# Window attention in a four-layer kernel: four heads side by side on groups of 32 array rows, scores formed twice, no transposes

## The reference

```python
win = pad(layer_norm(x)) cut into 14x14 windows        # 16x16 padded to 28x28: 4 windows an image, 196 places each
q, k, v = split(win @ qkv_w + qkv_b)                   # 12 heads of 16 channels
attn = einsum('nqc,nkc->nqk', q, k) * 0.25
attn = attn + (q . rel_pos_h)[..., :, None] + (q . rel_pos_w)[..., None, :]
o = einsum('nqk,nkc->nqc', softmax(attn), v)
x = x + o @ proj_w + proj_b
x = x + gelu(layer_norm(x) @ fc1_w + fc1_b) @ fc2_w + fc2_b
```

## Time and profile before

| what | us |
|---|---|
| median of 3 runs | 423.51 (423.33 to 425.48) |
| the profiled execution, its own time | 425.65 |
| its span | 423.9 |
| first attention: relative terms done to first matmul of fc1 | 42.9 to 144.0 |
| second attention: the same | 234.7 to 335.7 |

### The profile page before, as it was taken

One profiled execution on the slowest core, in us unless ns is written; L12 is line 12 of the kernel. 1 busy time (PEld: TensorE's weight loads), 2 busy tenths in 40 slices (PEclk: granted clock), 3 DMA queues, 4 the chain that ended last, 5 costly groups with the idle time before them and its releaser, 6 DMA issues.

```text
span 423.9 us, 7574 instructions
## 1 busy us (share of the span) xinstructions
PE 395.2 (93%) x2686; PEld 310.0 (73%) x2686; DVE 216.7 (51%) x631; ACT 206.2 (49%) x708; POOL 151.1 (36%) x197
## 2 busy tenths in 40 slices
PE   5499669999999999999999759999999999999997
PEld 2149668888888646977958758888888646986656
DVE  6843238777776810134763228776776800141272
ACT  1042238998888443013042328898888453021220
POOL 9441027776665630000042018776666300000000
PEclk9999959999999999999999959999999999999999
DMA  6616999200000102010005970000000000000002
GB/s 161 93 13 126 140 169 252 50 2 2 2 2 0 39 0 55 3 57 0 2 0 109 148 123 2 2 2 2 2 1 2 2 0 0 2 0 2 0 1 76
DMA packets 8424, 17.42 MB, mean 41 GB/s; under 512 B 1909, under 2 KB 5430, under 8 KB 8386
## 3 DMA queue, kind: packets, MB, share of 16 engines
q1 hardware_dynamic: 8386, 16.93, 20.6%
HBM read 9.68 MB, written 0.79 MB: 25 GB/s over the span
## 4 chain that ended last, share of the span: by engine, by line
PE 86%; DMA 7%; DVE 5%; issue 0%; ACT 0%; SPq 0%
PE bank L658 16%; PE bank L734 9%; PE bank L687 8%; PE bank L743 7%; DMA qaug<-arena 6%; PE bank L613 6%; PE bank L712 5%; PE bank L626 5%; PE bank L665 4%; PE bank L664 3%; DVE norm_or_q L1101 3%; PE bank L586 2%; PE bank L903 2%; PE bank L832 2%; PE bank L842 2%; PE bank L756 2%
## 5 line engine op out<-in xcount | busy, mean ns | idle before, releaser
L545 POOL TENSOR_TENSOR probs<-probs,recip 98x392 f32<-98x392 f32 x96 | 80.6, 840 | 34.6 <-DVE recip L1163 33.9
L968 ACT ACTIVATE probs<-bank,negmax 98x196 f32<-98x196 f32 x192 | 80.5, 432 | 9.8 <-DVE negmax L1152 9.4
L658 PE MATMUL bank<-kaug,qaug 100*98 100x196 f32 x384 | 81.1, 334 | 0.0
L1152 DVE TENSOR_REDUCE negmax<-bank 98x2 f32<-98x392 f32 x96 | 53.7, 559 | 23.1 <-PE bank L658 23.1
L658 PEld LDWEIGHTS bank<-kaug,qaug 100*98 100x98 f32 x384 | 55.6, 164 | 7.3 <-ACT probs L968 5.0
L547 POOL TENSOR_SCALAR probs<-probs,recip 112x112 f32<-112x112 f32 (+1 forms) x48 | 28.0, 583 | 62.2 <-DVE recip L1163 60.7
L687 PE MATMUL bank<-ident,probs 98*98 98x98 f32 x384 | 47.5, 247 | 0.2
L687 PEld LDWEIGHTS bank<-ident,probs 98*98 98x98 f32 x384 | 40.2, 127 | 4.2 <-issue 0.5
L734 PE MATMUL bank<-yT,fc 96*128 96x512 f32 x96 | 41.9, 593 | 0.0
L968 ACT ACTIVATION_READ_ACCUMULATOR probs<-bank,negmax 98x1 f32 x192 | 40.9, 213 | 0.0
L973 ACT ACTIVATE probs<-bank,negmax 112x280 f32<-112x280 f32 (+1 forms) x48 | 24.5, 511 | 25.0 <-DVE negmax L1156 23.6
(11 more groups left out here) (151 smaller groups left out, 604.0 us busy)
## 6 DMA issues: line engine op xcount, KB each, us to landing
fc<-in_fc SPq DMA_DIRECT2D x4, 576.0 KB, 9.3
kaug<-arena SPq DMA_DIRECT2D x6, 346.0 KB, 4.4
qaug<-arena SPq DMA_DIRECT2D x4, 448.0 KB
qaug<-norm_or_q SPq DMA_DIRECT2D x24, 64.0 KB, 2.4
qaug<-arena SPq DMA_DIRECT2D x4, 224.0 KB
qkv<-in_qkv SPq DMA_DIRECT2D x2, 432.0 KB, 8.2
x_tok<-in_x SPq DMA_DIRECT2D x4, 192.0 KB, 3.6
inverse<-in_inverse SPq DMA_DIRECT2D x1, 768.0 KB
```

The lines of the kernel that those rows point to most:

```text
L545: pool.tensor_tensor(p, p, by.unsqueeze(2).broadcast_to([n, 2, cols // 2]), ALU.mult).then_inc(s.normed, 1)
L658: last = mm(bank[0:HALF_WIN, 2 * HALF_WIN * part:2 * HALF_WIN * (part + 1)], q[:, at:at + HALF_WIN], keys, start=True, stop=True)
L968: ins = run(m.probs[0:HALF_WIN, slot, cols], bank[0:HALF_WIN, cols], ACT.Exp, bias=m.negmax[0:HALF_WIN, slot, part:part + 1], accum_out=m. ...
L1152: ins = dve.tensor_reduce(m.negmax[0:HALF_WIN, slot], bank[0:HALF_WIN, 0:4 * HALF_WIN].rearrange("k (a n) -> k a n", a=2), AX, ALU.max, ne ...
```

## The change

The attention is rewritten. Four heads form a slot (three slots), and each head has a group of 32 array rows: 16 rows of q or k with 16 zero rows, so that two slots can share one k tile. The relative terms have a tile of their own, `m.r`, with 28 rows for a head, one row for the negated maximum and one for a mask. A group of the new loop is four heads on one window set: 12 main and 6 edge groups a layer (`GROUPS`).

For a group, `score` forms queries by keys in banks 0 to 3, one head a bank: for a main group two blocks of 128 queries (all 256 places of the image), each as a product with k and one with the 0/1 table of keys, four heads side by side on the four row groups. `take_max` takes all maxima in one instruction and turns them with four 32x32 transposes on `dve`; `sp` moves them into row 28 of `m.r` (two small DMAs for a main group). `turn` then forms the scores again with keys first in banks 4 to 7, with the maximum already subtracted by that row, `act` takes exp of each bank, and `weigh` multiplies with v, whose 16 columns of ones give the sums. `take_weighed` copies the sums beside the outputs, inverts them for all 128 rows and 196 queries, and multiplies. There are no transposes on `pe`, no multiplication on `pool`, no copies of transposed blocks and no assembly DMAs; `pool` prepares the tiles of the edge groups instead. `out_project` has three products per tile instead of two, and `load_late` is issued as soon as the qkv weights have landed.

```diff
-UNITS = [(IMAGES + s, 4 * q + n) for q in range(QUADS) for s in range(2) for n in range(4)]
-UNITS += [(b, h) for b in range(IMAGES) for h in range(HEADS)]
-N_UNITS = len(UNITS)
...
+RIGHT_WIN, LOW_WIN = IMAGES, IMAGES + 1
+GROUPS = [(slot, b) for slot in range(2) for b in range(IMAGES)]
+GROUPS += [(slot, b) for slot in range(SLOTS) for b in (RIGHT_WIN, LOW_WIN)]
+GROUPS += [(SLOTS - 1, b) for b in range(IMAGES)]
+N_GROUPS = len(GROUPS)
+AHEAD = 3
+P_RING = 2
+M_RING = 3
...
-                            sp.dma_start(m.kaug[0:BIAS_ROW, quad, :], m.qkT[rows, chunk]).then_inc(s.aug[quad], 16)
...
-                        sp.dma_start(m.qaug[lo:lo + HD, head, :], m.qW[HD * n:HD * (n + 1), chunk]).then_inc(s.aug[head // 4], 16)
...
-                        sp.dma_start(m.qaug[lo:lo + WIN, heads, :], src[REL_ROWS[kind][g], g]).then_inc(s.aug_bias[g], 16)
...
+                wait_for(sp, s.proj_in, *taken_out(job("c", 2, 1)))
+                for j in range(4):
+                    sp.dma_start(m.k[GROUP * j:GROUP * j + HD, 1], m.k[GROUP * j + HD:GROUP * (j + 1), 1]).then_inc(s.k_moved, 16)
+                sp.wait_ge(s.edge_inputs, R_EDGES)
+                for n, (slot, b) in enumerate(GROUPS):
+                    sp.wait_ge(s.maxT, 4 * (n + 1))
+                    for part in range(max_moves(b)):
+                        n_max = 96 if part == 1 else 128
+                        if b < IMAGES:
+                            at = PLACES * b + 128 * part
+                            dst = m.r[MAX_ROW::GROUP, slot, at:at + n_max]
+                        else:
+                            dst = m.edgeR[MAX_ROW::GROUP, slot, b - IMAGES, :]
+                        sp.dma_start(dst, m.negmaxT[4 * part:4 * part + 4, n % M_RING, 0:n_max]).then_inc(s.max_rows[n % M_RING], 16)
             out_dram = out.rearrange("b h w c -> b (h w) c").rearrange("b (t p) c -> b p t c", p=128)
...
+                elif kind in ("rel_h", "rel_w"):
+                    if g == 0 and kind == "rel_h":
+                        pe.wait_ge(s.loaded["rel"], 16)
+                        for chunk in (0, 2):
+                            wait_for(pe, s.proj_in, *taken_out(job("c", chunk, 1)))
+                    for n in range(2):
+                        at = 2 * g + n
+                        for quad in range(4):
+                            q = m.q[row(quad)].rearrange("k s (b r w) -> k s b r w", b=IMAGES, r=SIDE)
+                            last = mm(bank[row(quad), 192 * n:192 * (n + 1)], wl["rel"][row(quad), 0 if kind == "rel_h" else 1, at % WIN],
+                                      q[:, :, :, at] if kind == "rel_h" else q[:, :, :, :, at], start=True, stop=True)
+                            if n == 1:
+                                last.then_inc(s.proj_in.pe, 1)
+                    return
...
+            def score(l, n, part):
+                s = A[l]
+                slot, b = GROUPS[n]
+                if part == 0:
+                    if n > 0:
+                        pe.wait_ge(s.max, n)
+                    else:
+                        wait_for(pe, s.proj_in, *taken_out(job("rel_w", SIDE // 2 - 1, 0)))
+                        pe.wait_ge(att_loaded, 16)
+                    if slot == SLOTS - 1:
+                        pe.wait_ge(s.k_moved, 16 * 4)
+                    if b >= IMAGES:
+                        pe.wait_ge(edges_loaded, 16 * 3)
+                        pe.wait_ge(s.edge_inputs, edge_ready(EDGES.index(n)))
+                for with_rel in (False, True):
+                    for j in range(4):
+                        if b < IMAGES:
+                            at = PLACES * b + 128 * part
+                            o = m.bank[j][:, MAIN_KEYS * part:MAIN_KEYS * (part + 1)]
+                            asking = (m.r if with_rel else m.q)[row(j), slot, at:at + 128]
+                            if with_rel:
+                                asked = c["keys"][row(j)].rearrange("k (r w) -> k r w", r=SIDE)[:, 0:WIN, 0:WIN]
+                            else:
+                                asked = inner(m.k[row(j), slot // 2])[:, b]
+                        else:
+                            e, keys = b - IMAGES, EDGE_KEYS[b - IMAGES]
+                            o = m.bank[j][0:queries(b), 0:keys]
+                            asking = queries_of(slot, b, j)[with_rel]
+                            asked = c["edge_keys"][row(j), e, 0:keys] if with_rel else m.edgeK[row(j), slot, e, 0:keys]
+                        last = mm(o, asking, asked, start=not with_rel, stop=with_rel)
+                        if with_rel and part == max_moves(b) - 1:
+                            last.then_inc(s.scores, 1)
+            def turn(l, n):
+                s = A[l]
+                slot, b = GROUPS[n]
+                if n == 0:
+                    for who in ("act", "dve"):
+                        wait_for(pe, s.proj_in, who, sum(p[3] == who for p in PROJ))
+                else:
+                    pe.wait_ge(s.probs, 4 * n)
+                if n >= 2:
+                    pe.wait_ge(s.weighed, attended(n - 2))
+                at, landed = max_landed(n)
+                pe.wait_ge(s.max_rows[at], landed)
+                cols = queries(b)
+                for tile in range(key_tiles(b)):
+                    for with_rel in (False, True):
+                        for j in range(4):
+                            last = mm(m.bank[4 + j][:, cols * tile:cols * (tile + 1)], keys_of(slot, b, j, tile)[with_rel],
+                                      queries_of(slot, b, j)[with_rel], start=not with_rel, stop=with_rel)
+                            if with_rel and tile == key_tiles(b) - 1:
+                                last.then_inc(s.turned, 1)
+            def weigh(l, n):
+                s = A[l]
+                slot, b = GROUPS[n]
+                pe.wait_ge(s.probs, min(4 * (n + 1) + 1, 4 * N_GROUPS))
+                cols, tiles = queries(b), key_tiles(b)
+                for tile in range(tiles):
+                    for j in range(4):
+                        last = mm(m.bank[weighed_in(n)][row(j), 0:cols], values_of(slot, b, j, tile), m.probsT[:, n % P_RING, j, cols * tile:cols * (tile + 1)],
+                                  start=tile == 0, stop=tile == tiles - 1)
+                        if tile == tiles - 1:
+                            last.then_inc(s.pv, 1)
...
+                pe.wait_ge(v_ones_set, 1)
+                for n in range(N_GROUPS):
+                    turn(l, n)
+                    ahead = n + AHEAD
+                    if ahead < N_GROUPS:
+                        score(l, ahead, 0)
+                    if n > 0:
+                        weigh(l, n - 1)
+                    if ahead < N_GROUPS and max_moves(GROUPS[ahead][1]) == 2:
+                        score(l, ahead, 1)
+                    for b in range(2):
+                        if n == OUT_AT[b] + 1:
+                            if b == 0:
+                                pe.wait_ge(s.loaded["late"], 16 * 3)
+                                pe.wait_ge(s.max, N_GROUPS)
+                            out_project(s, wl, b)
+                weigh(l, N_GROUPS - 1)
+                out_project(s, wl, 2)
+                pe.wait_ge(s.weighed, attended(N_GROUPS - 1))
...
+                            ins = run(m.q[:, slot, 512 * part:512 * (part + 1)], bank[:, :], ACT.Identity,
+                                      scale=c["slot_cols"][:, slot:slot + 1], bias=m.q_bias[:, l, slot:slot + 1])
...
+                for n, (slot, b) in enumerate(GROUPS):
+                    act.wait_ge(s.turned, 4 * (n + 1))
+                    if n >= P_RING:
+                        act.wait_ge(s.pv, 4 * (n - P_RING + 1))
+                    cols = queries(b) * key_tiles(b)
+                    for j in range(4):
+                        run(m.probsT[:, n % P_RING, j, 0:cols], m.bank[4 + j][:, 0:cols], ACT.Exp).then_inc(s.probs, 1)
...
+                        if g == 2:
+                            dve.tensor_scalar(m.q[:, 2, cols], bank[:, :], c["slot_cols"][:, 2:3], m.q_bias[:, l, 2:3], ALU.mult, ALU.add)
+                        ins = dve.tensor_scalar(m.k[:, g - 1, cols], bank[:, :], wl["vecs"][:, 6 + g:7 + g], None, ALU.add)
+                    elif kind == "rel_w":
+                        if g == 0:
+                            dve.wait_ge(s.proj_in.act, taken_out(job("rel_h", SIDE // 2 - 1, 0))[1])
+                        at = m.r[:, :, :].rearrange("k s (n w) -> k w (s n)", w=SIDE)[:, 2 * g:2 * g + 2]
+                        ins = dve.tensor_tensor(at, bank[:, 0:2 * 192].rearrange("k (w n) -> k w n", w=2), at, ALU.add)
...
+                def take_max(n):
+                    slot, b = GROUPS[n]
+                    at = m.negmax[:, n % 2]
+                    dve.wait_ge(s.scores, 4 * (n + 1))
+                    if b < IMAGES:
+                        dve.tensor_reduce(at[:, 0:8].rearrange("k (a j) -> k j a", a=2),
```

(32 more changed lines are left out.)

705 lines of the change are left out of this document (279 added, 426 removed).

## The result

The changed kernel takes **494.24 us** (median of 4 runs, 492.79 to 497.06) against 424.14 us for the kernel before on the same chip: a ratio of 1.166, 95% interval 1.159 to 1.173. The prediction was 466, range 428 to 503. Direction and range hold; the size is 28 us short. The profiled execution took 495.44 us, span 493.7.

A forecast was written before the change was run, and what follows sets the result against it. TensorE, 93% busy, bounds the old kernel; in the new rounds a chain through one VectorE does. 425.65 + 38.4 (19.2 a layer) + 3.5 for the clock = 467.6, 2.1 above the median: 466 us, range 428 to 503.

The forecast's parts named there:

- clock charge of the tails: Each layer's tail, TensorE waiting some 4.4 us for the norm: half of a 3.5 us loss charged, +3.5 in all.
- The reciprocal: VectorE's inversion of the sums for 196 columns: 1.52 us, at 7 ns a column from two small rows.
- fast reciprocal: Rival: VectorE's inversion is no slower than a copy, a round takes 4.7 us, total 432 us; chance 0.09.
- The ring: Attention round: first score block, product and handoff 1.75, weighed step 2.27, reduction 1.78; total 5.8 us where 5.0 stood.
- W: VectorE's weighed step in each round, copying the sums, inverting and multiplying: 2.27 us.
- Row groups side by side: TensorE's products on four row groups run together as on column groups: 0.67 a score block, 1.33 for turned scores.
- Against: such short gaps cost nothing before; only one of 6.8 did.: Argument against a clock fall from TensorE's two idle places a round, 1.5 to 2 us.
- all-or-nothing rival: The clock falls in the attention loop: rounds of 8.6 us, +50 to 55 a layer, 574 us; chance 0.05.
- Relative terms: ... as now: Each layer's relative terms before attention: 128 products in four-wide passes, 64 x 0.16 = 10.3 us, unchanged.
- The four transposes: VectorE's small transposes of the maxima, about 0.1 us each, lying beside the round's chain.
- The start: Stretch before the first layer's relative terms, forecast to begin at 34.2 us.
- the other side: Rival: weighed step 1.1 us, weight loads run ahead, shorter handoffs, no clock loss in the tail: 419 us; chance 0.06.

The follow-up runs named there:

- fill run: The changed kernel with six extra products a round in TensorE's idle place ahead of the turned scores, changing no result: 484.54 us.
- order run: The changed kernel with the products of group n - 1 issued ahead of the first score block of group n + 3 instead of behind it: 470.07 us.

## Why the prediction was right, and where it was short

By the sum's own steps, for the profiled executions (495.44 measured, 467.6 forecast, 27.8 short):

| step | forecast | measured, first and second layer | miss, both |
|---|---|---|---|
| start of the first relative terms | 34.2 | 25.86 | -8.4 |
| relative terms | 10.3 | 15.75, 15.75 | +10.9 |
| their end to the fifth maximum | 22.6 | 23.9, 25.6 | +4.3 |
| to the last maximum (13 rounds) | 71.4 | 80.0, 80.1 | +17.3 |
| to the last weighed step | 17.8 | 19.4, 19.3 | +3.1 |
| norm, to fc1 | 6.7 | 8.5, 9.4 | +4.5 |
| clock charge of the tails (now in the two rows above) | 3.5 | | -3.5 |

What is left over, under half a us, lies between the layers. Cut by cause and not by stretch, the half-clock stretches in the rounds make 19 of the 27.8 us and the strided reads 10.3; the early start takes 8.4 back, and the remaining 7, net of the 3.5 charged for the clock, are mostly in the head and the norm, where half-clock stretches fall too (272.2, 169.8 and 398.5). That the start offset most of the strided reads is luck. That the time fell in the range is not: its upper end, 503, had been drawn for a clock that falls in part of the rounds.

- **The reciprocal.** 1.52 us forecast for 196 columns, 1.38 measured; 0.95 and 0.85 for 128 and 112, so 6.3 ns a column and not 7. The slope from two tiny rows decided most of the size of the forecast (466, against 432 with a fast reciprocal), and the price from it was good to 10%. The repeat count that the Trainium skill gives ("VectorE: DVE Perf Modes", walkthrough of the pipeline) pointed rightly to a slow operation; the 8.3 ns a column that the prediction estimated from it was too much here.
- **The ring.** First block, products, W 2.27, reduction 1.78 gave 5.8: measured 5.84 with W 2.1, reduction 1.78 and handoffs a little longer. The run without the inversion shows that it decides.
- **Row groups side by side.** Taken as equal to column groups: 0.163 to 0.167 for four records, no 1.3. The 8 us that the prediction estimated from the 3.07 times of the Trainium skill ("TensorE: Matmul & The Clock Gate", Part 3) are not seen for unit steps.
- **"Against: such short gaps cost nothing before; only one of 6.8 did."** This is the step that failed. I priced the clock as an all-or-nothing rival, at 0.05, and the truth was a part of it: rounds at 5.84 for some 25 us, then half-clock stretches in six of a layer's rounds, each 1.4 to 1.7 us longer. The idle places of 1.56 us did cost nothing; those of 2.44 us in the rounds without a second score block, which the prediction did not tell apart, cost 9.5 us a layer with what followed them. The kernel before had no such place round after round, so its rows could not speak for harmlessness; what the prediction quoted from the Trainium skill ("TensorE: Matmul & The Clock Gate", Part 1), that the gate follows how busy TensorE is, was nearer. The fill run removes the stretches from the rounds, the order run all but one a layer.
- **"Relative terms: ... as now".** The count of passes was right, and read without a stride they take 10.6 us where 10.3 was forecast; the price of a pass was not, since half the jobs step through the moving operand 64 bytes at a time. The step itself is not new. The kernel before read its widths by the same 64-byte steps, 64 columns for each weight load of 112, and there they cost little: its first width records start 0.112 us apart, its height records 0.098. Why so little there no run asks. With 192 columns and weights of 32 columns the same step doubles the pass, and I had one price for both kinds.
- **The four transposes**, "each like other tiny operations, about 0.1": 0.89 for four. It was hidden: one in their place left the rounds at 4.43.
- **The start** came 8.4 us earlier. The four normalising operations ahead of the first projection take 1.25 us where they took 9.19, which is nearly all of it. I had costed the removed clearing at nothing, without asking whom it had held up. That the clearing made those 7.9 us is likely, but not shown: put back in another form it gave 2.1.

The rivals: the fast reciprocal and the other side needed W near 1.1, and it was 2.1; even without the inversion the time was 436. A better form of this design exists, with the bank freed early, the order changed and the strided reads gone, but it only draws level, at 0.999.

## What to carry to other kernels

Work that leaves TensorE still has to fit the ring it joins: write down, for every loop, the chain of engines from one buffer's release to the next, and count in it whatever stands ahead in the same queue, as the inversion did twice here. Idle places of TensorE can cost twice, once for the time and once for the clock: here places of 1.56 us in every round did not, places of 2.44 us did, and splitting or filling them brought the clock back. So look at the rounds that lack a piece of work, not only at the common one. When an operand is read in steps, price it from rows of that step and that shape: a step that cost a seventh in one shape doubled the pass in the other.
